# Gathers that read their indices where the lists of edges, slots and rows lie, without a copy per batch, in a kernel for two graph networks

## The reference

```
h = relu(layernorm(x));  x = x + gnn0(h, src, dst)
h = relu(layernorm(x));  x = x + gnn1(h, rows=src, cols=dst)

gnn0:  h1 = relu(h @ Wp1.T + bp1)
       p1 = pool_max(h1)                       # segment_max of h1[src] over dst, 0 where no edge
       x  = relu([h, p1] @ Wm1.T + bm1)
       x  = layernorm(relu([x, pool_max(x)] @ Wm2.T + bm2) + x)
       x  = layernorm(relu([x, pool_max(x)] @ Wm3.T + bm3) + x)

gnn1:  q, k, v = h @ Wq + bq, h @ Wk + bk, h @ Wv + bv      # 8 heads of 32
       s = (q[rows] * k[cols]).sum over a head
       out = softmax of s over the edges of a row, times v[cols], summed by row;  out @ Wo + bo
```

## Time and profile before

| | us |
|---|---|
| median of 3 runs | 5759.88 |
| the three runs, least and greatest | 5755.8 and 5779.17 |
| the profiled execution, its time | 5784.07 |
| the profiled execution, span from first to last instruction | 5782.3 |
| the passes lie at about | 127 to 1248, 1384 to 2482, 2608 to 3710 |
| the attention lies at about | 3988 to 5632 |

### The profile page before, as it was taken

How to read it: one execution, slowest core, us unless ns; L and a number is a source line. 1 busy time by engine, 2 the same in 40 slices (tenths; PEclk the granted TensorE clock), 3 DMA queues, 4 the chain that set the end, 5 groups by cost and what they waited for, 6 DMA issues and landing times. The chain is left out here.

```text
span 5782.3 us, 24077 instructions
## 1 busy us (share of the span) xinstructions
PE 1135.6 (20%) x4114; PEld 729.4 (13%) x4114; DVE 3373.5 (58%) x7030; ACT 429.5 (7%) x1091; POOL 3624.6 (63%) x3767
## 2 busy tenths in 40 slices
PE   3333311116223201061222000185000000000005
PEld 3222211114111100041111000153000000000003
DVE  4666666654444443363455333375777777777776
ACT  3000000002000000030000000042000000000001
POOL 1676666746666676646767766523766666666653
PEclk9555555558555555585555555597555555555557
DMA  4555555535555555555556555535656666666653
GB/s 131 174 190 181 185 179 190 192 128 167 190 198 188 199 196 186 188 176 190 194 195 206 197 180 184 168 122 162 201 169 189 187 189 187 188 190 189 189 173 102
DMA packets 341065, 1039.46 MB, mean 180 GB/s; under 512 B 73625, under 2 KB 140966, under 8 KB 307504
## 3 DMA queue, kind: packets, MB, share of 16 engines
q0 software_dynamic: 209536, 613.51, 36.1%
q1 hardware_dynamic: 131376, 424.41, 19.9%
HBM read 649.96 MB, written 388.08 MB: 180 GB/s over the span
## 5 line engine op out<-in xcount | busy, mean ns | idle before, releaser
L473 POOL DMA_INDIRECT G<-tab,ix x2349 | 2297.6, 978 | 1001.7 <-issue 687.1
L503 DVE SCALAR_TENSOR_TENSOR G<-G,reset 128x256 f32<-128x256 f32 x2349 | 1065.2, 479 | 1485.3 <-DMA G<-tab,ix 737.3
L1448 POOL DMA_INDIRECT kv<-kvtab,ix x936 | 884.4, 945 | 285.0 <-issue 285.0
L1446 POOL DMA_INDIRECT q<-qtab,ix x234 | 221.0, 945 | 415.6 <-remote 192.8
L1564 PE MATMUL trio<-ident,state 128*128 128x128 f32 x6 | 1.9, 426 | 1681.7 <-DVEq L1586 1681.7
L595 PE MATMUL tail<-ident,h 128*128 128x128 f32 x294 | 94.0, 421 | 1184.2 <-DVE U L564 471.6
L1468 DVE TENSOR_TENSOR kv<-kv,wide 128x3072 f32<-128x3072 f32 x78 | 260.8, 3344 | 26.9 <-issue 21.3
L1470 DVE TENSOR_REDUCE s<-kv 128x96 f32<-128x3072 f32 x78 | 261.5, 3353 | 2.7
L860 PE MATMUL trio<-hot 128*128 128x196 bf16 x783 | 143.0, 366 | 541.6 <-DVE hot L839 243.2
L1275 POOL DMA_INDIRECT pool<-hist,nix x147 | 139.3, 948 | 121.6 <-DVE nix L1281 70.8
L1564 PEld LDWEIGHTS trio<-ident,state 128*128 128x128 f32 x6 | 1.2, 219 | 1682.5 <-DVEq L1586 1682.5
(11 more groups left out here) (323 smaller groups left out, 3603.7 us busy)
## 6 DMA issues: line engine op xcount, KB each, us to landing
hist<-G SPq DMA_DIRECT2D x261, 1152.0 KB
G<-tab,ix POOLq DMA_INDIRECT x2349
ahist<-state SPq DMA_DIRECT2D x78, 408.0 KB
tab<-o SPq DMA_DIRECT2D x147, 128.0 KB
kv<-kvtab,ix POOLq DMA_INDIRECT x936
h<-tab SPq DMA_DIRECT2D x98, 128.0 KB
G<-tab SPq DMA_DIRECT2D x98, 128.0 KB
kvtab<-okv SPq DMA_DIRECT2D x49, 256.0 KB
```

The costliest lines, as they stand in the source:

```text
L473: g.indirect_dma_start(G[b][:, k, :], None, tab, bass.IndirectOffsetOnAxis(ix[:, b, k:k + 1], 0)).then_inc(s_eg[b].sem, 16)
L503: ins = v.scalar_tensor_tensor(out=G[b][:, k, :], in0=before, scalar=reset[:, at:at + 1], in1=G[b][:, k, :], op0=ALU.add, op1=ALU.max)
L1446: g.indirect_dma_start(qs[b][:, r, :], None, qtab, bass.IndirectOffsetOnAxis(ix[:, b, R * SLOT + r:R * SLOT + r + 1], 0)).then_inc(s_query ...
L1448: g.indirect_dma_start(kvs[b][:, k, :], None, kvtab, bass.IndirectOffsetOnAxis(ix[:, b, k:k + 1], 0)).then_inc(s_eg[b].sem, 16)
```

## The change

The tile `ix`, its semaphore and all copies into it are gone. Each gather takes its index as a column of the list itself: `src_ix` in a pass, `row_node` and `dst_ix` in the attention. Since the copies were also what held GpSimd back, their place is taken by other waits:
- In a pass, fold 2 counts up a new semaphore `c_taken`, and gather n waits for fold 2 of batch n-2: then fold 0 to 2 have taken what they need of buffer n-3. The wait for the store stays. Fold 5, which needs fold 2, now waits for `c_taken` in place of `chain`.
- In the attention, the query gathers wait for ScalarE's copy of batch n-3 (`c_query`) and the gathers of keys and values for the pairs (L1493, now L1492) of batch n-3, which count up `c_taken`. The instruction behind, L1496 (now L1495), needs the pairs too and waits for `c_taken` besides `chain`.

The core of the diff:

```diff
@@ max_pass, GpSimd
+            def edge(n, k):
+                return k % C * (CH // C) + n * STEPS + k // C
...
                     def gather(i, b):
-                        g.wait_ge(c_eix.sem, c_eix.of(i, b, UB))
+                        if i * UB + b >= 2:
+                            g.wait_ge(c_taken.sem, c_taken.of(i, b - 2, UB))
                         g.wait_ge(s_hs[b].sem, s_hs[b].base + i * 16)
                         for k in range(J):
-                            g.indirect_dma_start(G[b][:, k, :], None, tab, bass.IndirectOffsetOnAxis(ix[:, b, k:k + 1], 0)).then_inc(s_eg[b].sem, 16)
+                            at = edge(i * UB + b, k)
+                            g.indirect_dma_start(G[b][:, k, :], None, tab, bass.IndirectOffsetOnAxis(src_ix[:, at:at + 1], 0)).then_inc(s_eg[b].sem, 16)
@@ max_pass, VectorE
-                    def place(b, n):
-                        if n < NB:
-                            v.tensor_copy(ix[:, b, 0:J].rearrange("p (j c) -> p c j", c=C),
-                                          src_ix[:, 0:CH].rearrange("p (c s) -> p c s", c=C)[:, :, n * STEPS:(n + 1) * STEPS]).then_inc(c_eix.sem, 1)
-                    for m in range(2):
-                        place(m, m)
...
                             if k == C - 1 and n:
                                 v.wait_ge(c_batch.sem, c_batch.of(i, b - 1, UB))
+                            elif k == 2 * C - 1:
+                                v.wait_ge(c_taken.sem, c_taken.of(i, b, UB))
                             elif j or n:
                                 v.wait_ge(chain.sem, done[k - C if j else k - C + J])
...
                             if k == J - 1:
                                 ins.then_inc(c_batch.sem, 1)
+                            elif k == C - 1:
+                                ins.then_inc(c_taken.sem, 1)
                             else:
                                 done[k] = chain.inc(ins)
-                            if k == 2 * C - 1:
-                                place((b + 2) % UB, n + 2)
@@ attention_pass, GpSimd
                     def gather(i, b):
-                        g.wait_ge(c_eix.sem, c_eix.base + times(i, b, 2))
+                        n = i * UB + b
+                        if i:
+                            g.wait_ge(c_query, times(i - 1, b, 1))
                         for r in range(R):
-                            g.indirect_dma_start(qs[b][:, r, :], None, qtab, bass.IndirectOffsetOnAxis(ix[:, b, R * SLOT + r:R * SLOT + r + 1], 0)).then_inc(s_query[b], 16)
+                            at = r * NBA + n
+                            g.indirect_dma_start(qs[b][:, r, :], None, qtab, bass.IndirectOffsetOnAxis(row_node[:, at:at + 1], 0)).then_inc(s_query[b], 16)
+                        if i:
+                            g.wait_ge(c_taken.sem, c_taken.of(i - 1, b, UB))
                         for k in range(R * SLOT):
-                            g.indirect_dma_start(kvs[b][:, k, :], None, kvtab, bass.IndirectOffsetOnAxis(ix[:, b, k:k + 1], 0)).then_inc(s_eg[b].sem, 16)
+                            at = (k % R * NBA + n) * SLOT + k // R
+                            g.indirect_dma_start(kvs[b][:, k, :], None, kvtab, bass.IndirectOffsetOnAxis(dst_ix[:, at:at + 1], 0)).then_inc(s_eg[b].sem, 16)
@@ attention_pass, VectorE, weigh
-                        chain.inc(v.tensor_tensor(pairs[:, :, :, :].rearrange("p a r f -> p (a r) f"), first, vals[:, HALF:2 * HALF, :], ALU.add))
+                        v.tensor_tensor(pairs[:, :, :, :].rearrange("p a r f -> p (a r) f"), first, vals[:, HALF:2 * HALF, :], ALU.add).then_inc(c_taken.sem, 1)
                         chain.link(v.tensor_tensor(state[b][:, :, D:ACC], held[:, :, D:ACC], z_row[:, :, :], ALU.add))
-                        place(b, i * UB + b + UB)
+                        v.wait_ge(c_taken.sem, c_taken.of(i, b, UB))
                         chain.link(v.tensor_tensor(held[:, :, 0:D], held[:, :, 0:D], pairs[:, 0, :, :], ALU.add))
```

More of the change, by code:

```diff
@@ L169, in gnn_kernel @@
         eps = sb(top, "eps", [P, 1])
-        ix = sb(top, "ix", [P, UB, R * SLOT + R], I32)
         nix = sb(top, "nix", [P, UN], I32)
@@ L201, in gnn_kernel @@
         s_hs = [Count(sem(f"s_hs{b}")) for b in range(UB)]
-        c_eix, c_batch, c_w, c_e = (Count(sem(n)) for n in ("c_eix", "c_batch", "c_w", "c_e"))
+        c_taken, c_batch, c_w, c_e = (Count(sem(n)) for n in ("c_taken", "c_batch", "c_w", "c_e"))
         s_held = {"vector": sem("s_held_v"), "pool": sem("s_held_p")}
@@ L501, in stage @@
                             before = G[b][:, k - C, :] if j else G[(b - 1) % UB][:, J - C + c, :]
-                            at = c * (CH // C) + n * STEPS + j
+                            at = edge(n, k)
                             ins = v.scalar_tensor_tensor(out=G[b][:, k, :], in0=before, scalar=reset[:, at:at + 1],
@@ L539, in _ @@
                     staged(a, NB, UB, fill + side.scalar(a, evac))
-            c_eix.close(NB)
+            c_taken.close(NB)
             c_batch.close(NB)
@@ L1452, in _ @@
                 def _(v):
-                    def place(b, n):
-                        if n < NBA:
-                            v.tensor_copy(ix[:, b, 0:R * SLOT].rearrange("p (e r) -> p r e", r=R), of_slot[:, :, n, :]).then_inc(c_eix.sem, 1)
-                            v.tensor_copy(ix[:, b, R * SLOT:R * SLOT + R], of_row[:, :, n]).then_inc(c_eix.sem, 1)
                     chain.link(v.memset(state[UB - 1][:, :, :], 0.0))
-                    for m in range(UB):
-                        place(m, m)
                     def score(i, b):
@@ L1523, in _ @@
                         sp.wait_ge(s_hs[b].sem, s_hs[b].base + (NBA // UB) * 16)
-            c_eix.close(2 * NBA)
+            c_taken.close(NBA)
             c_batch.close(NBA)
```

## The result

The changed kernel takes **5808.94 us** (median of 7 runs, 5781.61 to 5823.65) against 5759.88 us before (7 runs), 1.0076 times as long, 95% interval 1.005 to 1.0102. It is slower, by 0.8%; forecast was 5580 us, 3% faster. The profiled execution has a span of 5820.0 us, 37.7 more than before.

What follows compares the result with a forecast made beforehand. No engine was full; GpSimd's waits above its gather floor were winnable, VectorE setting the attention's pace. Passes -135, attention -40, stage starts -5 make -180: 5784.1 to 5604, less 24.2 for the median, 5580 us; range 5440 to 5750.

Steps and rivals of the forecast that it cites:

- The floor: GpSimd's gathers: least time 1.27 us each in passes (995 us a pass), 1.25 in the attention (1463 us); idle above it winnable.
- the far end of -490: Passes and attention: 490 us won if all of GpSimd's waits before gathers, about 297 and 192.8 us, were recovered.
- So some 3.5 us of each such stall stays won: Passes: releasing at fold 2 keeps 3.5 of 4.8 us per stall; 75, 40 and 20 us by pass, -135 together.
- The copies themselves at 0: Passes: removing 261 VectorE copies, 44 us at most, wins nothing; in a slow turn at most half a step, 0.70 us.
- Attention, -40 us: Attention: two copies fewer and one wait more per batch win 0.55 us a batch, 40 us; bounds 12 and 162 us.
- rival 1: Attention: the copies are what late results wait for, so it gives 162 us rather than 40; 5458 us, chance 0.20.
- the price of a wait: Attention: an instruction that waits costs 1.40 us in the slow turn, and the change adds one wait before L1496.
- I am wrong at the root if passes 1 and 2 win less than pass 3: Passes: sign that the place of L564, ahead of the old release in passes 1 and 2 only, did not decide.
- Rival 4: Attention: a wait costs more than a copy, +98 us, and the passes give only 50; 5808 us, chance 0.10.
- Rival 3: Passes: TensorE's late product makes the stalls, VectorE cannot catch up and waits only shift; 5745 us, chance 0.10.
- Rival 2: Stores and VectorE take over the waits: passes give 40 us, attention 12; 5705 us with the starts, chance 0.14.
- The rule on shared ports: Passes: VectorE instructions with two SBUF inputs contend with GpSimd reading SBUF; by it the sum would be 60 us less.

Runs made afterwards that it cites:

- e5: Changed kernel, release back at fold 5, plus a one-element VectorE copy between L1493 and L1495 in each attention batch: 5795.67 us, 1.0005 of the kernel before.
- e6: Changed kernel, release back at fold 5, attention maximum taken in one VectorE instruction, so 14 instead of 15 a batch: 5752.59 us, 0.993 of the kernel before.
- e11: e6 with the attention's key and value gathers bringing 1 KB rows from the queries' table instead of 2 KB: 5755.73 us, 0.9941 of the kernel before.
- e16: e6 with the attention's twelve key and value gathers made on 64 partitions instead of 128: 5745.58 us, 0.9959 of the kernel before.
- e7: e6 with the two halves of the weighted values made by one instruction, so 13 VectorE instructions a batch: 5758.03 us, 0.9943 of the kernel before.
- e8: Changed kernel, release back at fold 5, GpSimd pausing every third batch of pass 1 for fold 2 of the batch before: 5753.31 us, 0.9935 of the kernel before.
- e15: Changed kernel, release back at fold 5, pass 1's gathers bringing 512-byte rows instead of 1 KB: 5746.33 us, 0.9968 of the kernel before.

## Why the prediction was wrong

**The floor.** The prediction took 1.27 and 1.25 us a gather as "the floor of a pass while GpSimd issues every gather", from a stretch of 100 us, and called the rest "idle time above the floor", 297 us in the passes and 192.8 in the attention. The floor over a whole stage is about 1.40 us a gather, and the rows read for the prediction already had it: busy and idle time over count are (770.9 + 338.4)/783 = 1.42 in pass 1, (760.3 + 339.9)/783 = 1.41 and (766.4 + 323.5)/783 = 1.39 in passes 2 and 3, and the attention's 1633.5 us over 1170 gathers are 1.40. The kernel before stood on this limit in every stage. After the change, pass 2, pass 3 and the attention have 1.40, 1.37 and 1.38. What lies under 1.40 is the start of a stage: in the attention some 180 gathers at 1.25 and 990 at 1.40 make 1611 us, and 1610.5 were measured. What a fast stretch gains is given back as a wait, a longer gather or a stall. In the changed attention GpSimd waits for nothing, but its gathers are longer (991 and 1332 ns at the mean instead of 945 from 4400 to 5400 us), and the mean is 1.40 still. This takes away the gain of the passes but for some us, and the far end of -490 with it.

**"So some 3.5 us of each such stall stays won"** is the step that made the sign wrong. It let VectorE stop "for 9.60 us" whatever GpSimd did. A long stall lasts until GpSimd stops, some 4 to 6 us past its last gather; freeing GpSimd for one batch more, 11.4 us, made the one shown 12.7 us longer (9.60 to 22.34), and the 13 waits of 8.3 us at the mean became 16 of 13.9. What was the effect of the stall, GpSimd's standing still for lack of the copy, was what ended most of them. Pass 1 then lost 87 us instead of winning 75. "I am wrong at the root if passes 1 and 2 win less than pass 3" was the right sign to look for: they won -87, 5 and 9 us.

**The copies themselves at 0.** In a slow turn the copy was worth a whole step: after the change the turns of pass 3 that were 14.0 us take 12.6, 9 folds at 1.40. The bound of "at most half of one step" was wrong, read off the distance to the neighbouring folds. It pays little, as 12.6 us is also what nine gathers take.

**Attention, -40 us.** It won 23, all of it in the first 25 batches: the stretch of 23.80 us a batch (17 instructions x 1.40) is gone, and 8 batches run at 18.8 where 3 did. From then on it is 21.0 us before and after. Neither rival 1 (162 us, the copies as cause of the late results) nor the price of a wait was right: with the copies gone, the three waits for own results still come to 193 us from 4400 to 5400 us (70.9, 54.0 and 68.3), where they were 200 before. In e5 an instruction without a wait costs a step, and in e6 the waits go with one instruction less.

**Rival 4**, slower, had the number (5808) by luck and nothing of the cause: it put the loss in the attention, which won 23 us, and a gain of 50 in the passes, which lost 73. Rival 3 (5745) named the late product as what makes the stalls, but it, too, took the 9.6 us as given. Rival 2, that stores and VectorE take over the waits, describes the idle time after the change best (169.8 us of pass 1's are ended by a store of hist), but as the outcome of the longer stall and not as a limit that was near.

**The rule on shared ports** (the Trainium skill, "SBUF — State Buffer", "Who interferes with whom") was set aside in the prediction by a pause that did not end the slow folds. The runs neither need it nor show it: the folds of a slow turn, with two SBUF inputs each, start 1.40 us apart, and in e5 a copy of one element made the batch longer by as much (22.4 us instead of 21.0); GpSimd's 1.40 us stay when VectorE has 14 or 13 instructions instead of 15.

## What to carry to other kernels

Take an engine's floor from a whole stage, (busy + idle)/count over hundreds of instructions, and compare stages: if all come out alike (here 1.39 to 1.42 us a gather), that is the limit, however much idle time stands beside it and however fast a short stretch is. When an engine waits for a count, look whether the work behind the count is late or only the count. Before an engine is freed to go on during another's stall, ask what ends the stall; if it ends when that engine stops, the release is worth less than nothing, and the place of a count (fold 5, behind the waiting instruction) can be what keeps it short. Where a price is one per instruction, fewer instructions are what is left to try; a kernel with fewer gathers was not run.

## What the runs showed of the hardware

- An indirect DMA of GpSimd costs 1.40 us in the long run and 1.25 us for the first ten or so batches of the attention; the difference is paid as longer gathers (1.24 to 1.8 us), pauses or stalls. In the attention it does not depend on bytes (2 KB or 1 KB rows, e11), on rows (64 or 128, e16) or on whether VectorE has 14 or 13 instructions a batch (e6, e7). Its cause is not shown.
- While GpSimd issues gathers without a break, the count of a product of TensorE reaches VectorE up to 25 us behind the product's last matmul in pass 1. The longest of these waits end 4 to 6 us after the last gather; pauses of 4 to 6 us every three turns prevent them (e8). Halving the gathers' bytes changes nothing (e15).
- VectorE, too, can fall to one instruction per 1.40 us at the mean of a batch or turn: 17 and 16 in batches of 23.80 and 22.40 us, 10 in turns of 14.00. That 15 take 21.00 us and 9 take 12.60 is no evidence of its own, since 15 and 9 gathers take as long. In e5 and in the kernel before it came out of that state again midway (16 and 17 instructions in 21.0 us); why was not found.
- In that state the updates of VectorE's own counts lie on a grid of 0.70 us, half of 1.40. From 3508 to 3526 us after the change they stand at 3509.1, 3510.5, 3511.2, 3513.3, 3514.7, 3515.4 and so on to 3525.9: all 13 lie whole multiples of 0.70 us apart. From 600 to 630 us before the change there is no such grid. So late results of VectorE and the late count of TensorE may have one cause: that is argued, not shown.
- Each execution on record has its span and granted clock from a trace. Whether tracing has a part in these delays, no run tells.
